# Shared weight loads for paired products, an earlier layer 0, edge products moved behind product 3, and stores spread out, in a chain of four modulated convolutions

## The reference, cut to what matters

```python
def _layer(x, style, w, b, mw, mb, typ):
    s = style @ mw.T + mb
    weight = SCALE * w * s[:, None, :, None]
    demod = lax.rsqrt(jnp.sum(weight * weight, axis=(2, 3)) + EPS)
    weight = weight * demod[:, :, None, None]
    ...
out = x
for i, typ in enumerate(('same', 'upsample', 'same', 'downsample')):
    out = _layer(out, style, weights[i], biases[i], mod_w[i], mod_b[i], typ)
x = x + out
```

## Time and profile before

| | us |
|---|---|
| median of three timed runs | 175.73 (174.91 to 176.23) |
| the profiled execution | 177.4 |
| its span, first to last instruction | 175.6 |
| PE busy in the span | 162.1 |
| VectorE, ScalarE, GpSimd busy | 136.0, 56.0, 84.0 |

### The profile page before, as it was taken

The page is one execution under the profiler, slowest core; times in us unless marked ns, Lnnn a source line. Parts: engine busy times, 40 slices in busy tenths (PEclk is TensorE's granted clock), DMA queues, the critical chain, the costliest instruction groups (busy, mean ns, idle before and its releaser), DMA issues. The chain is left out here.

```text
span 175.6 us, 8950 instructions
## 1 busy us (share of the span) xinstructions
PE 162.1 (92%) x4015; PEld 147.4 (84%) x4015; DVE 136.0 (77%) x239; ACT 56.0 (32%) x126; POOL 84.0 (48%) x138
## 2 busy tenths in 40 slices
PE   7999879979998899999899999999999999999960
PEld 5688766969767589899798999989899999999940
DVE  7639972789599598979496878787879797979992
ACT  3244533405113133333323233424242424231110
POOL 7009905218064081939173646464647473748400
PEclk9999978999999999999999999999999999999998
DMA  4970000030300301249082633333333343030332
GB/s 127 344 116 0 6 0 4 4 119 7 119 4 6 119 6 30 97 192 292 5 279 89 235 127 123 123 123 123 123 123 123 123 123 123 4 122 5 122 127 120
DMA packets 9382, 17.81 MB, mean 101 GB/s; under 512 B 4704, under 2 KB 5248, under 8 KB 9344
## 3 DMA queue, kind: packets, MB, share of 16 engines
q1 hardware_dynamic: 9280, 17.22, 28.7%
q10 hardware_dynamic: 64, 0.02, 0.1%
HBM read 8.85 MB, written 8.39 MB: 98 GB/s over the span
## 5 line engine op out<-in xcount | busy, mean ns | idle before, releaser
L187 POOL TENSOR_TENSOR Hw<-Hw 128x192 f32<-128x192 f32 x15 | 9.0, 600 | 67.3 <-DVE Hw L791 67.3
L458 PE MATMUL p_m<-uu,Hw 64*64 64x128 f32 x992 | 31.7, 268 | 0.0
L378 PE MATMUL p_lo<-xin,w0s 64*64 64x259 f32 x384 | 28.3, 407 | 1.9 <-DVE e_sb L817 1.9
L458 PEld LDWEIGHTS p_m<-uu,Hw 64*64 64x64 f32 x992 | 29.6, 132 | 0.0
L423 PE MATMUL p_le<-R_sb,F_st 64*64 64x128 f32 (+2 forms) x768 | 27.2, 275 | 1.2 <-issue 1.1
L378 PE MATMUL p_le<-xin,w0s 64*64 64x260 f32 x384 | 26.9, 391 | 0.0
L423 PEld LDWEIGHTS p_le<-R_sb,F_st 64*64 64x64 f32 x768 | 24.5, 139 | 1.9 <-issue 1.9
L448 PE MATMUL p_m<-u,Hw 64*64 64x256 f32 x384 | 25.8, 375 | 0.0
L802 DVE TENSOR_TENSOR uu<-u 128x516 f32<-128x516 f32 x32 | 23.8, 792 | 1.5
L654 ACT ACTIVATE u<-p_lo 128x518 f32<-128x518 f32 x16 | 9.7, 604 | 45.6 <-PE p_lo L378 45.6
L254 POOL COPY Hw<-Hw 64x896 f32<-64x896 f32 x15 | 23.6, 1575 | 0.9
(11 more groups left out here) (133 smaller groups left out, 216.5 us busy)
## 6 DMA issues: line engine op xcount, KB each, us to landing
xin<-in_x_dram SPq DMA_DIRECT2D x16, 512.0 KB, 4.3
out_dram<-ot SPq DMA_DIRECT2D x16, 512.0 KB, 3.1
wn<-in_L_cond_weights_dram SPq DMA_DIRECT2D x1, 192.0 KB, 3.3
mwn<-in_L_cond_mod_w_dram SPq DMA_DIRECT2D x1, 128.0 KB, 2.2
xe<-in_x_dram SPq DMA_DIRECT2D x2, 56.0 KB, 8.6
cn<-in_cond_dram ACTq DMA_DIRECT2D x1, 16.0 KB, 2.0
bn<-in_L_cond_mod_b_dram ACTq DMA_DIRECT2D x1, 1.0 KB
bn<-in_L_cond_biases_dram ACTq DMA_DIRECT2D x1, 1.0 KB
```

The source lines that it names most:

```text
L378: ins = pe.matmul(bank[h * C:(h + 1) * C, s, 0:n], w0s[p % 2][rows, k, :], xin[p % NX][rows, i0:i0 + 2 * n - 1:2], start=(k == 0), stop=(k ...
L458: ins = pe.matmul(bank(h)[s * C:(s + 1) * C], tap(p, h, s, blk), moving(slice(h * C, (h + 1) * C), s, k), start=(k == 0), stop=(k == len(b ...
```

## The change

Weights: `wn` is held twice side by side (`wn2`, two loads from DRAM), and `mwT`, `wsumT` and `o_st` are written twice by ScalarE. A product that was issued as two matmuls for the two halves of the partitions is now one with 128 columns of weights. The copies that make `V_st` go from ScalarE to GpSimd.

Order ahead of the loop: the transposition of `wsum` comes ahead of `style`; `layer0_odd(1)` and `compose_H(1)` ahead of the constants `zc` and `oc`; `edge_x0` between these two; `layer0_even(1)` behind them. On VectorE `make_diffs(0)` comes ahead of `a0`.

In the loop: `compose_R` is no longer behind PE's waits for the edges; `edge_y`, `edge_z` and `edge_out` stand at the end of iterations 0, 1 and 2, and their VectorE parts between `finish` and `add_x`. SP's stores and loads get new waits. For the last but one pair `add_x` is done by ScalarE (scale) and GpSimd (add).

```diff
-        wn = sb("wn", [C, LAYERS, C, K])
+        wn2 = sb("wn", [C, LAYERS, 2, C, K])
+        wn = wn2[:, :, 0]
...
-            sp.dma_start(wn[:], weights.rearrange("l o i k -> o l i k")).then_inc(w_loaded, 16)
+            for h in range(2):
+                sp.dma_start(wn2[:, :, h], weights.rearrange("l o i k -> o l i k")).then_inc(w_loaded[h], 16)
...
             def taps_transposed(l, bank, c0):
                 for k in range(K):
-                    for h in range(2):
-                        ins = pe.matmul(bank[h * C:(h + 1) * C, c0 + k * C:c0 + (k + 1) * C],
-                                        wn[:, l, :, k], ident[0:C, 0:C], start=True, stop=True)
+                    ins = pe.matmul(bank[:, c0 + k * C:c0 + (k + 1) * C], taps(l, k), ident[0:C, 0:C],
+                                    start=True, stop=True)
...
+            pool.wait_ge(made["wsum"], 1)
+            pool.wait_ge(zeroed, 7)
+            V = wn[:, 2].rearrange("o i k -> o k i")
+            pool.tensor_copy(V_st[0:C], V).then_inc(copied["V_st"], 1)
+            pool.wait_ge(copied["V_st"], 1)
+            pool.tensor_copy(V_st[C:P], V).then_inc(copied["V_st"], 1)
...
+                if p in (LATE, LATE + 2, LATE + 4):
+                    sp.wait_ge(m2_done, p + 1)
+                    store(n)
+                    n += 1
                 if p + 4 < PAIRS:
-                    sp.wait_ge(H_done, min(p + 3, PAIRS))
+                    sp.wait_ge(mid_done, p + 1)
                     load(p + 4)
-
-                if LATE - 1 <= p < 2 * LATE - 2:
-                    store(2 * (p - LATE + 1))
-                    sp.wait_ge(H_done, p + 4)
-                    store(2 * (p - LATE + 1) + 1)
-                if p >= 2 * LATE - 2:
-                    store(p)
+                if p >= LATE - 1:
+                    if p < PAIRS - 2:
+                        sp.wait_ge(out_made, p + 1)
+                    store(n)
+                    n += 1
...
+            layer0_odd(1)
+            compose_H(1)
+
             pe.wait_ge(made["z_st"], 6)
             pe.wait_ge(made["yc"], 1)
             pe.wait_ge(copied["w2T"], 1)
...
+                product_1_mid(p)
+                product_3(p)
                 if p < 3:
                     pe.wait_ge(s_made, p + 1)
                 if p == 0:
-                    edge_x0()
+                    edge_y()
                 if p == 1:
-                    edge_y()
+                    edge_z()
                 if p == 2:
                     edge_out()
-                product_1_mid(p)
-                product_3(p)
-                if p == 1:
-                    edge_z()
...
+            p = PAIRS - 2
+            act.wait_ge(z_made, 2 * (p + 1))
+            for h in range(2):
+                act.activation(z_sb[p % 2][:, h], z_sb[p % 2][:, h], ACT.Copy, scale=pcol(W_D3, p)).then_inc(z_scaled, 1)
...
+            p = PAIRS - 2
+            n = (L - 2 * EDGE) // 2
+            pool.wait_ge(stored[p % NO_T], 16 * (p // NO_T))
+            for h in range(2):
+                i0 = EDGE + h * n
+                pool.wait_ge(z_scaled, h + 1)
+                pool.tensor_tensor(ot[p % NO_T][:, i0:i0 + n], z_sb[p % 2][:, h, h:h + n],
+                                   xin[p % NX][:, i0 + 1:i0 + 1 + n], ALU.add).then_inc(x_added, 1)
```

More of the change, by code:

```diff
@@ new lines, in _ @@
+            ts(vec[:, V_B0, 0:B], dm[:, 1, :], bias[:, 0:1], name="vec")
+            make_uu(0)
+            demodulation(3, 4)
+            ts(vec[:, V_SB1, 0:B], style[:, 2, :], bias[:, 1:2])
+            sum_taps(0)
+            then()
+            dve.wait_ge(put["yc"], 1)
+            tt(yc[:], p_m2[:, 0, 0:B], vec[:, V_E1, 0:B], ALU.mult)
+            then()
+            stt(yc[:], vec[:, V_SB1, 0:B], 2.0, yc[:], ALU.mult, ALU.add, "yc")
+            sum_blocks(dve, 0)
+            dve.wait_ge(H_sums, 3)
```

267 lines of the change are left out of this document (133 added, 134 removed).

## The result

The changed kernel takes 177.81 us (median of 20 runs, 175.95 to 180.88), the one before 176.25 (20 runs, 174.91 to 178.66): a ratio of 1.0069, 95% interval 1.0041 to 1.0096. It is 0.7% slower, where 167.3 was forecast. Medians here are of all timed runs of a kernel; a ratio is of those of its runs that lie within 1.5% of its fastest, since some runs come out some per cent longer.

The account below looks back on a forecast made before the run. PE, busy 92% of the span, was taken as the bound, gains coming only from its longer stretches. Terms -2.2 - 4.4 - 1.6 - 0.2 = -8.4 us, from the median 175.73 to 167.3 us; range 164.0 to 171.5.

Parts of the forecast that it names:

- Merged products, forecast 0: Seven groups of small products, half the matmuls at double price: no gain; other end about 1.6 us lower.
- Half as many at double price is no gain: Ground for costing the merging at 0: 64-column products 0.125 us each, 128-column ones 0.25.
- Bounds: -0.35 ... +0.6: Range for compose_H(0)'s start: -0.35 if small operations run without GpSimd in their way, +0.6 if not and copies are late.
- signs of being wrong: Small 128-column products clearly under 0.2 us, a second clock fall, PE idle for x0e or oe, holes beside single transfers.
- sign of being right: A granted clock of 1.00 throughout the start, one of several signs listed.
- Start of the program, +0.25: Before compose_H(0): wsumT's wait saved, lost again to VectorE's make_diffs(0) ahead of a0; start at 18.55 instead of 18.30.
- Between compose_H(0) and product 2 of pair 0, -2.45 in all: PE's yc gap -1.85, clock fall -1.5, oc product -0.25, edge product of x0 +0.95, new wait +0.1; product 2 at 28.7.
- Up to +0.9 if GpSimd's sums of the same moment lengthen VectorE's small operations: Upper bound on PE's new wait for edge_x0 before product 2 of pair 0, costed at +0.1.
- Edges behind product 3, -4.4: Pairs 0 to 2 take 29.64 us against 34.01, as PE asks for edges 3.3 us later; bounds -3.4 to -4.7.
- Waiting stores, -1.6: Stores of pairs 0 to 3 spaced out remove most of 2.16 us excess in three later pairs; bounds 0 and -2.1.
- Tail, -0.2: Pair 14's add_x leaves VectorE, which ends 0.9 us earlier; the end lies between 0.7 later and 0.6 earlier.
- The collision that I feared: In the tail, VectorE's add_x(15), two operands in SBUF, holds up GpSimd's second addition; the end is 0.7 us later.

Follow-up runs that it names:

- unmerged: The changed kernel with its merged products issued again as pairs of 64-column halves, everything else as changed; 171.66 us, ratio 0.9774 to the kernel before.
- single: The changed kernel with halves, one load of the weights, tiles held once and wsumT behind the taps; 170.87 us, ratio 0.9708 to the kernel before.
- the rows with both halves in one place: The kernel before with blocks of small products added; pairs of 64-column loads into the same half took 0.44 us at clock 0.50; whole run 224.24 us.
- tail back: The single kernel with add_x(14) on VectorE again; 171.9 us, ratio 0.9721 to the kernel before.
- mended: The single kernel with W_D3 and V_D3 copies behind edge_x0 and later output edge steps in pair 3; 169.52 us, ratio 0.9589 to the kernel before.
- the best one: The single kernel with W_D3 and V_D3 copies behind edge_x0 and later output edge steps on ScalarE and GpSimd; 167.52 us, 0.9530 of the kernel before.
- the edges put back: The single kernel with the three edge products of pairs 0 to 2 back between compose_H and product_1_mid; 171.33 us, ratio 0.9706 to the kernel before.

## Why the prediction was wrong

**Merged products, forecast 0: the step that failed.** "Half as many at double price is no gain" set 0.125 us for 64 columns (6.39 to 7.39) against 0.25 for 128 (23.26 to 24.01). Both numbers were read rightly and don't belong together. The first group ran at TensorE's low speed: 0.25 us for two halves is near the 0.23 that they take at a clock of 0.50, and in eight profiles of kernels with halves (unmerged, single and others) the same group takes 0.58 to 0.59 us in all, 0.147 for two. In the single one:

```profile
6.08 0.66 PE L373 MATMUL p_m<-cT,mwT 128*64 128x32 f32 x16 [0.35 <-ACT mwT L647]
6.67 0.74 PE L337 MATMUL p_m<-ident,wn 64*64 64x64 f32 x12
```

The second ran at the high speed, where 128 columns take 0.225 to 0.25. At one speed two halves cost 0.13 against 0.225, or 0.23 against 0.43. Twenty products ahead of compose_H(0) are merged ones: at half speed that costs 0.20 us each, 4.0 in all as an estimate, and the kernel before with the merging and the second load starts compose_H(0) 4.49 us later. The forecast thus compared halves at half speed with wholes at full speed, and the factor of two vanished. The whole sum was then 4.2 us too low at this place; the bound on that side ("Bounds: -0.35 ... +0.6") held nothing of it, and no rival did. Among the signs of being wrong the forecast named only small products that take under 0.2 us for 128 columns; they took more, and what was missing was the pair of halves at 0.13. And its sign of being right, a granted clock of 1.00 throughout the start, came true in the record while the products ran at the low speed. The Trainium skill's page "TensorE: Matmul & The Clock Gate", section "LDWEIGHTS (loading the stationary operand)", that I named as agreeing gives the time of one load, and the rows with both halves in one place bear it out; it says nothing of two that overlap.

**Start of the program, +0.25.** Without the merging this came out better: compose_H(0) starts at 17.70 in the runs whose start is of the same kind as before's (tail back and mended), 0.60 sooner than 18.30. The bound on the lower side was -0.35. But these kernels have no second load, and wsumT in its old place; the two cost 0.5 us between unmerged and single, so that of the changed order about -0.1 is left (an estimate), better than forecast and inside the bounds.

**Between compose_H(0) and product 2 of pair 0, -2.45 in all: right but for one term.** It came to -0.52 in the changed kernel and to -2.14 in the mended one, where the wait for x0e is gone. The gap and the fall of the clock behind it went. "Up to +0.9 if GpSimd's sums of the same moment lengthen VectorE's small operations" was the danger, and it was under-priced: the operations collided with GpSimd's copies and not with its sums, and the wait became 1.27 us in the changed kernel and 1.60 in the single one. Without it product 2 of pair 0 starts at 28.18 in the mended one; 28.7 was forecast.

**Edges behind product 3, -4.4.** Measured -3.33 in the changed kernel, where a hole of about 0.7 us fell into pair 2 (10.19 us against 9.47 in the single one), and -4.1 in the best one (29.92 us for the three pairs, 29.64 forecast). The size was right, but the reason was in part another, as the edges put back show: over pairs 0 to 3 (42.58 us before, 40.73 with the edges put back, 38.46 in the best one) 1.85 us are edge_x0's leaving and one edge a pair, 2.3 the later place. That VectorE's lateness is paid back within the 1.5 us of air in a pair was wrong for the last edge: +0.94 in pair 3. The steps of oe take 3.1 us (0.53 + 1.10 + 1.04 + 0.44), partly beside GpSimd's copies, in place of the 1.75 that I took from ye.

**Waiting stores, -1.6.** The profiles before and after had 0.6 of it (87.6 and 87.0 us). Timed against its own undoing it is 1.6 in one pair of kernels and 0.9 (ratios) to 2.0 (medians) in another, and the averages over the profiles differ by 1.4. The size was about right. That stores make the holes is borne out by the runs with small stores; that a fetch is what waits is not shown, and against the runs stands "a fetch then waits for one transfer at most, as in the plain pairs, which have no such hole": behind single stores there are holes too.

**Tail, -0.2.** It gave 0.6; GpSimd's additions took 1.26 each and VectorE's add_x 1.39 beside them, in place of 1.28. The collision that I feared cost 0.1.

So the forecast of 167.3 was that of a kernel without the merging and without two waits: that one exists and takes 167.52. That the two agree so closely is partly luck, since by its profile compose_H(0) starts 2.1 us sooner than forecast, most of it from the quicker kind of start, and the other terms together came out less than forecast. Of the 10.3 us between it and the changed kernel the merging with its load and wsumT's new place is the greater part (5.1 us at the start of compose_H(0), 22.79 against 17.70 in starts of the same kind), and the rest is the wait for x0e (1.3), pair 3 (0.9) and what differs between starts.

## What to carry to other kernels

- Two small products whose weight loads go to different halves of TensorE's columns run beside each other (0.13 us for both, 0.225 for one of twice the columns). Don't merge them, however many instructions it saves.
- Before two rows are set against each other as prices, bring both to the same speed of the engine: find in each stretch a group whose full-speed time is known. The recorded clock alone may not say it.
- A stage moved to an engine "with 1.5 us of air in a pair" needs less than that in every pair it enters, with its operations at the length that they have beside GpSimd's copies. If it doesn't fit, move it to an engine that waits; into the next pair it only takes the wait along.
